# Far blocks' relative terms as rows of one product, and routed rows scattered to their tokens: a Macaron layer on one core

## The reference, cut to what matters

```python
x = x + 0.5 * ffn(layernorm(x), ...)          # x: 16 sequences x 512 tokens x 128
x = x + attention(layernorm(x), ...)
x = x + 0.5 * ffn(layernorm(x), ...)

def attention(hidden_states, ...):            # 16 heads of 8
    dist = jnp.clip(arange(s)[:, None] - arange(s)[None, :], -128, 128) + 128
    rel_pos = rel_emb[dist]
    scores = einsum('bhqd,bhkd->bhqk', q, k) + einsum('bhqd,qkd->bhqk', q, rel_pos)
    attn = softmax(scores / sqrt(8))
    local_ctx = einsum('bhqk,bhkd->bhqd', attn, v)
    ...                                       # a linear global part, gated; then Wo

def ffn(x_aD, ...):                           # 8192 tokens, 8 experts, F = 256
    topv, topi = top_k(x_aD @ router_DE, 2)
    gates = sigmoid(scores of the two chosen experts, -inf elsewhere)
    for each expert e: out_e = (silu(g x W_in[e]) * (g x W_swiglu[e])) @ W_out[e]
    return shared_ffn(x_aD) + sum over e of out_e
```

## Time and profile before

| | |
|---|---|
| median of three runs | 2360.72 us |
| the profiled execution | 2373.01 us |
| its span, first to last instruction | 2371.2 us |
| granted TensorE clock, mean | 0.934 |
| busy: PE, VectorE, ScalarE, GpSimd | 2056.5, 1517.5, 1417.9, 1163.2 us |
| phases: load and ffn1, attention, ffn2 | 0 to 480, 480 to about 1835, 1835 to 2371 us |

### The profile page before, as it was taken

How to read it: one execution, slowest core, us unless ns; L and a number is a source line. 1 busy time by engine, 2 the same in 40 slices (tenths; PEclk the granted TensorE clock), 3 DMA queues, 4 the chain that set the end, 5 groups by cost and what they waited for, 6 DMA issues and landing times. The chain is left out here.

```text
span 2371.2 us, 49029 instructions
## 1 busy us (share of the span) xinstructions
PE 2056.5 (87%) x16104; PEld 1440.3 (61%) x16104; DVE 1517.5 (64%) x4212; ACT 1417.9 (60%) x2771; POOL 1163.2 (49%) x1525
## 2 busy tenths in 40 slices
PE   4777899849999999999999999999999777799850
PEld 3555677626666666666666666666665555667640
DVE  7775556636767767776766666666664766555641
ACT  3655566626666666666667666666774555566540
POOL 0776004446665656555654545455531277400676
PEclk9878999958999999999999999999999888999985
DMA  5355878668887888888878888888882114677862
GB/s 133 128 195 205 243 238 260 215 175 235 237 234 231 242 224 247 241 236 230 250 222 233 247 244 241 229 239 244 240 240 78 32 51 161 193 242 242 269 202 75
DMA packets 293456, 493.53 MB, mean 208 GB/s; under 512 B 42452, under 2 KB 196948, under 8 KB 293204
## 3 DMA queue, kind: packets, MB, share of 16 engines
q1 hardware_dynamic: 237364, 309.26, 46.8%
q0 software_dynamic: 53248, 180.01, 23.5%
q10 hardware_dynamic: 2592, 1.13, 0.2%
HBM read 252.56 MB, written 210.89 MB: 195 GB/s over the span
## 5 line engine op out<-in xcount | busy, mean ns | idle before, releaser
L1422 DVE CUSTOM_DVE_ANT_0 at_junk<-at_ps_s,at_rel 128x512 bf16<-128x512 f32 x1024 | 664.5, 686 | 238.0 <-PE at_ps_s L978 209.6
L1153 ACT ACTIVATE at_probs<-at_ps_t 128x512 f32<-128x512 f32 x1024 | 558.0, 598 | 94.1 <-PE at_ps_t L963 81.5
L1162 ACT COPY at_src<-at_ps_r 128x512 f32<-128x512 f32 x512 | 302.1, 590 | 360.9 <-PE at_ps_r L992 258.0
L963 PE MATMUL at_ps_t<-tab_ident,at_rel 128*128 128x128 f32 x3328 | 483.8, 285 | 0.0
L963 PEld LDWEIGHTS at_ps_t<-tab_ident,at_rel 128*128 128x128 f32 x3328 | 361.2, 143 | 69.3 <-issue 2.0
L509 POOL DMA_INDIRECT rows_x<-ffn_xe,rows_index x256 | 263.7, 1030 | 180.7 <-ACT ffn_xe L461 103.1
L519 POOL DMA_INDIRECT ffn_zg<-rows_z,rows_home x176 | 177.0, 1006 | 349.4 <-issue 349.4
L720 DVE TENSOR_TENSOR ffn_h<-ffn_silu,ffn_ps_gate 128x512 f32<-128x512 f32 x248 | 170.5, 687 | 259.7 <-ACT ffn_silu L482 259.1
L1006 PE MATMUL at_ps_v<-at_probs,at_v 128*32 128x256 f32 x4096 | 330.6, 395 | 0.2 <-ACT at_probs L1153 0.2
L978 PE MATMUL at_ps_s<-at_ks,at_qs 31*128 31x512 f32 x1024 | 307.6, 504 | 3.9 <-DVE at_mx L1422 2.3
L482 ACT ACTIVATE ffn_silu<-ffn_ps_mid 128x512 f32<-128x512 f32 x248 | 148.8, 600 | 243.9 <-PE ffn_ps_gate L321 243.4
(11 more groups left out here) (204 smaller groups left out, 3438.1 us busy)
## 6 DMA issues: line engine op xcount, KB each, us to landing
at_band<-at_src POOLq DMA_DIRECT2D x192, 574.0 KB, 4.9
at_rel<-at_band SPq DMA_DIRECT2D x512, 143.5 KB
ffn_w_expert<-rows_w SPq DMA_DIRECT2D x92, 768.0 KB, 5.1
at_band<-at_src POOLq DMA_DIRECT2D x64, 512.0 KB, 5.1
ffn_xg<-rows_x SPq DMA_DIRECT2D x92, 256.0 KB, 3.9
rows_z<-ffn_y SPq DMA_DIRECT2D x92, 256.0 KB, 5.4
rows_x<-ffn_zero SPq DMA_DIRECT2D x46, 256.0 KB, 3.2
at_rel<-at_band SPq DMA_DIRECT2D x64, 128.0 KB
```

The costliest lines, as they stand in the source:

```text
L963: ins = pe.matmul(ps_t[:, i, HALF * n + P * l:HALF * n + P * (l + 1)], rel[:, c % RREL, l, 2 * hp + i, kb * P:(kb + 1) * P], ident[:], sta ...
L1153: act.activation(probs[:, kp, 2 * hp + i].rearrange("p n q -> p (n q)"), ps_t[:, i, :], ACT.Exp).then_inc(exp_done.sem, 1)
L1162: act.copy(src[:, l, 2 * hp:2 * hp + 2, 0:BAND], ps_r[:, :, 0:BAND]).then_inc(qr_out.sem, 1)
L1422: dve.tensor_tensor_reduce(out=junk[:, i, :], in0=ps_s[:, i, :], in1=rel[:, c % RREL, l, h, :], scale=1.0, scalar=-3e38, op0=ALU.add, op1= ...
```

## The change

It has two parts.

**Attention.** For the first two query blocks, the far keys to the right (distance clipped at the other end) get their relative term from the stack. One product per sequence of the queries with a table `wf` (the difference of the two end rows, by head; three matmuls of 16 x 256) gives the term for 256 queries and 16 heads; VectorE splits it into a high and a low part in the unused rows of `k32`, and SP sends it by four transfers into spare rows of `qs`, for which `ks` has ones from the first far key on. The transposes of the far blocks are skipped, `fill_far` stops at the end of the near blocks, and the rest of `rel` is zero. The far product takes V's place at (2, 2); V goes to (3, 3) and its copy to (4, 0).

**FFN.** Every row sent to an expert carries one more number, the row of `rows_t` at which its output belongs (token and choice; rows of padding have a spare number). In ffn2 VectorE takes these numbers from the loaded tile (`take_ids`), GpSimd scatters `y` with them, four indirect DMAs of 128 rows per job (`scatter_out`), instead of SP's store; and SP loads the tiles back by two plain transfers (`load_back`), tiles 0 to 9 in the last jobs, 10 to 15 after them. ffn1 carries the numbers too but gathers as before.

```diff
+                t = n - FIRST_B[1] - 7
+                return t if n < JOBS and GROUPS[0][0] <= t < GROUPS[0][1] else None
...
+            return 16 * 2 * (T if first else 1) * (t // RZ + 1)
+
+        def z_written(n):
+
+            return 16 * (1 if first else T) * (b_of(n) // 2 + 1)
...
+                    if not first:
+                        sp.wait_ge(ids_done, b_of(n - RG) + 1)
...
+            def load_back(t):
+
+                last = FIRST_B[0 if t < CUT else 1] + TILES[0 if t < CUT else 1] - 1
+                for n in (last - 1, last):
+                    sp.wait_ge(z_out[n % 2], z_written(n))
+                if t >= RZ:
+                    sp.wait_ge(z_added, t - RZ + 1)
+                for k in range(2):
+                    at = k * TOKENS + t * W
+                    sp.dma_start(zg[:, t % RZ, k], rows.t[at:at + W].rearrange("(p c) d -> p c d", p=P)).then_inc(z_in[t % RZ], 16)
...
-                if NA <= n - 4 < JOBS:
+                if first and NA <= n - 4 < JOBS:
                     store_rows(n - 4)
+                if not first and gathered_at(n + 1) is not None:
+                    load_back(gathered_at(n + 1))
                 if store is not None and gathered_at(n - 1) is not None:
                     store_result(gathered_at(n - 1))
             if store is not None:
-                for t in LATE:
+                for t in LATE[:RZ]:
+                    load_back(t)
+                for i, t in enumerate(LATE):
                     store_result(t)
+                    if i + RZ < len(LATE):
+                        load_back(LATE[i + RZ])
...
-                    act.wait_ge(z_out[m % 2], 16 * (b_of(m) // 2))
+                    act.wait_ge(z_out[m % 2], z_written(m - 2))
...
+                    act.copy(xe[:, t % RX, :, :, D:D + 1].rearrange("p k s a -> p k (s a)"), ids[:, t])
...
+            def scatter_out(n):
+                pool.wait_ge(y_done, b_of(n) + 1)
+                pool.wait_ge(ids_done, b_of(n) + 1)
+                for c in range(T):
+                    pool.indirect_dma_start(rows.t, bass.IndirectOffsetOnAxis(row_ids[:, n % RI, c, :], 0),
+                                            y[:, n % 2, c, :], None).then_inc(z_out[n % 2], 16)
...
+            else:
+                for n in range(NA, JOBS):
+                    scatter_out(n)
...
+            def take_ids(n):
+                dve.wait_ge(rows_in[n % RG], 16 * rows_loads(n))
+                if b_of(n) >= RI:
+                    dve.wait_ge(z_out[n % 2], z_written(n - RI))
+                drawn = xg[:, n % RG, :, D:D + 1].rearrange("p c a -> p (c a)")
+                dve.tensor_scalar(beside[:, n % RI], drawn, float(2 * TOKENS), float(W * (n % RI)), ALU.is_ge,
+                                  ALU.mult).then_inc(ids_step, 1)
+                dve.wait_ge(ids_step, b_of(n) + 1)
+                dve.tensor_tensor(row_ids[:, n % RI].rearrange("p c a -> p (c a)"), drawn, beside[:, n % RI],
+                                  ALU.add).then_inc(ids_done, 1)
...
-    PROJECT_V, V_OUT = (2, 2), (2, 3)
+    PROJECT_V, V_OUT = (3, 3), (4, 0)
     QUERIES_IN = ((2, 0), (2, 0), (2, 1))
     KEYS_IN = ((3, 0), (3, 1), (3, 0))
+    FAR_PROJECT, FAR_OUT, FAR_IN = (2, 2), (2, 3), (3, 0)
...
-                            if kb < qb - 1:
+                            if kb < qb - 1 or kb > qb + 1:
...
+                    far_ring, n = seq_ring(far_in, c // PER)
+                    pe.wait_ge(far_ring.sem, far_ring.at(n + 1, 0))
...
+                    pe.wait_ge(far_done.sem, far_done.at(b, 2))
+                elif slot == 4 and b is not None:
...
+                elif place == FAR_PROJECT:
+                    pe.wait_ge(qlo_done.sem, qlo_done.at(b, 1))
                     pe.wait_ge(k32_done.sem, k32_done.at(b, 1))
                     maximum_left(c)
                     if e is not None:
                         pe.wait_ge(o_step.sem, o_step.at(e, 8))
+                    for i, (w, q) in enumerate(((wf_hi, q_hi), (wf_hi, q_lo), (wf_lo, q_hi))):
+                        ins = pe.matmul(misc[0:H, 0:HALF], w[:], q[:, 0:HALF], start=(i == 0), stop=(i == 2))
+                    ins.then_inc(far_prod.sem, 1)
+                elif place == PROJECT_V:
+                    pe.wait_ge(far_done.sem, far_done.at(b, 2))
+                    maximum_left(c)
+                    if e is not None:
+                        pe.wait_ge(g_step.sem, g_step.at(e, 6))
...
-                            pe.wait_ge(v_done.sem, v_done.at(coming(c), 1))
+                            pe.wait_ge(far_done.sem, far_done.at(coming(c), 2))
...
-                        pool.tensor_copy(rel[:, c % RREL, l, :, key:S],
-                                         far[:, c % RREL, l].broadcast_to([P, HG, S - key])).then_inc(fill_done.sem, 1)
+                        end = P * (2 * half_of(c) + l + 2)
+                        pool.tensor_copy(rel[:, c % RREL, l, :, key:end],
+                                         far[:, c % RREL, l].broadcast_to([P, HG, end - key])).then_inc(fill_done.sem, 1)
...
+                if place == FAR_IN:
+                    sp.wait_ge(far_done.sem, far_done.at(b, 2))
+                    far_ring, r = far_in[b % R2], b % R2
+                    for x in range(4):
+                        l, part = x // 2, x % 2
+                        at = (STEP * x + STEP - 1) * LINE + r * SETS * S + P * l
+                        to = bass.AP(qs[:].tensor, at, [[32 * LINE, HG], [S, SETS], [1, P]])
+                        src_at = HALF * part + P * l
+                        sp.dma_start(to.bitcast(F32), k32[0:H, src_at:src_at + P]).then_inc(far_ring.sem, 16)
...
+            for x in range(4):
+                far_from = HALF + P * (x // 2)
+                ones = bass.AP(ks[:].tensor, (STEP * x + STEP - 1) * LINE + far_from, [[32 * LINE, HG], [S, R2 * SETS], [1, S - far_from]])
+                sp.dma_start(ones.bitcast(F32), glob[0:32, 2:2 + (S - far_from) // P, :]).then_inc(extra_in.sem, 16)
...
+                elif place == FAR_OUT:
+                    high, low = (k32[0:H, HALF * part:HALF * (part + 1)].bitcast(F32R) for part in range(2))
+                    dve.wait_ge(klo_done.sem, klo_done.at(b, 1))
+                    dve.wait_ge(far_prod.sem, far_prod.at(b, 1))
+                    dve.tensor_copy(high, misc[0:H, 0:HALF]).then_inc(far_done.sem, 1)
+                    dve.wait_ge(far_done.sem, far_done.at(b, 1))
+                    dve.tensor_tensor(low, misc[0:H, 0:HALF], high.bitcast(F32), ALU.subtract).then_inc(far_done.sem, 1)
...
+                                dve.memset(rel[:, j, 0, :, 2 * P:S], 0.0).then_inc(rel_cleared.sem, 1)
                                 dve.memset(rel[:, j, 1, :, 0:P], 0.0).then_inc(rel_cleared.sem, 1)
+                                dve.memset(rel[:, j, 1, :, 3 * P:S], 0.0).then_inc(rel_cleared.sem, 1)
...
-        rows.x.append(dram(f"rows_x{g}", [tall, D]))
+        rows.x.append(dram(f"rows_x{g}", [tall, D + 1]))
         rows.z.append(dram(f"rows_z{g}", [(2 * tiles + E - 1) * ROWS_AT_ONCE, D]))
+    rows.t = dram("rows_t", [(2 * sum(GROUP_TILES) + 8) * ROWS_AT_ONCE, D])
```

103 lines of the change are left out of this document (70 added, 33 removed).

## The result

| | before | after |
|---|---|---|
| median of the runs | 2361.48 us (4 runs, 2360.05 to 2362.70) | 2323.91 us (4 runs, 2320.92 to 2326.26) |
| the profiled execution | 2373.01 us, span 2371.2 | 2320.92 us, span 2319.1 |
| ratio of the medians | | 0.984, interval 0.9817 to 0.9863 |

The change makes the kernel 37.6 us faster; 62 were predicted, and the range of 2262 to 2330 us holds the result. Two of the four executions of experiment 6, which took 2586.72 and 3327.58 us at granted clocks unlike the others, are left out everywhere.

What follows compares the result with a forecast made beforehand. Attention was taken as bound by TensorE's work, the second FFN's 80 us tail by GpSimd's gathers. Gains of 27 us in attention and 35 in the FFN made 62: 2360.7 - 62 = 2299 us, range 2262 to 2330.

Steps and rivals of the forecast that it cites:

- The upper bound of 83 us: Attention, even items: 768 transposes fewer at 0.108 us each save at most 83 us, with no stall coming in.
- 0.85 us a pair: Attention, last two steps of even items: each shortened pair saves 0.85 us, 54 us over 64 pairs.
- What is given back, 27 us in sum: Attention: costs of 6, 7, 9, 3 and 2 us taken off the 54 us saved, leaving 27 gained.
- Local outputs, 6 us: Attention, step 2 of slots 0 and 2: VectorE's reciprocal and product cost 0.2 us in 30 pairs, 6 us (0 to 16).
- Far rows on the band product's wait, 9 us: Attention, first step of slot 4: the next sequence's band products wait for four more transfers, 15 x 0.6 = 9 us.
- Low part of the keys, 3 us: Attention, early sequences: VectorE's far product copy out of PSUM waits for the keys' low part, 3 us (0 to 10).
- Late pieces, 7 us: Attention, step 3 in the first 68 slots: VectorE's additions cost 0.2 us in 34 pairs, 7 us (0 to 20).
- Collision at the start of the second stage, 9 us: Second FFN: the third output waits for the first one's scatters, behind GpSimd's first-stage sends; 9 us lost on ScalarE.
- Loads and stores in the last jobs, 5: Second FFN: group 0's ten direct loads and their stores fall in the last ten jobs, costing 5 us (0 to 12).
- The last rows land 14 us after the last output was due, and 17 for the tail: Second FFN's end: scatters lag closely spaced last jobs, 14 us (8 to 20); loading six tiles back, 17 (14 to 24).
- Rival C: Second FFN, second stage: scatters held by VectorE take 1.96 us each and bound it; slower, 2383 us, chance 0.04.
- Rival A: Attention gives nearly nothing: VectorE's loop and ScalarE set short steps, relative rows arrive late; gain 5 + 35, 2321 us, chance 0.13.

Runs made afterwards that it cites:

- experiment 6: The changed kernel with each query block's band sent out by two transfers of two heads: 2292.66 and 2315.18 us, no ratio given.
- 3: The kernel before with the far transposes left out and nothing in their place: 2521.46 us, ratio 0.9961 to the kernel before.
- 12: The changed kernel with the far transposes done all the same, adding zeros: 2495.78 us, ratio 0.9893 to the kernel before.
- 9: The changed kernel with the band sent in two transfers of two heads, run again on another chip: 2470.26 us, ratio 0.9813 to the kernel before.
- 11: The changed kernel with four output buffers instead of two in both FFN phases, on a third chip: 2467.20 us, ratio 0.9769 to the kernel before.
- 2: The kernel before with all FFN edits and none of the attention's: 2502.91 us against 2530.54, ratio 0.9889.
- 7: The kernel before with the band sent in two transfers of two heads: 2392.59 us, ratio 1.012 to the kernel before.
- 1: The kernel before with all attention edits and none of the FFN's: 2523.98 us against 2530.54, ratio 0.9955.
- 4: The changed kernel with four output buffers instead of two in both FFN phases, on the first of its chips: 2485.07 us, ratio 0.9832 to the kernel before.
- 5: The changed kernel once more, unedited, on another chip: 2322.67 us against 2364.28 for the kernel before, ratio 0.9806.
- 10: The changed kernel with the band in two transfers and four output buffers in both FFN phases: 2455.59 us, ratio 0.975 to the kernel before.
- experiment 8: The changed kernel with ScalarE's exponent of each step ahead of its half of the band copy: 2514.17 us, ratio 1.0626 to the kernel before.

## Why the prediction was right or wrong

### Where the attention's gain went

**The steps at full clock.** A sequence has 32 steps, eight slots of four, and each of them can be followed through the sequences: from one pair of score products to the next. At full clock the median length of a step agrees between the kernels to some 0.01 us wherever the edits don't touch it; step 3 of slots 4 and 7 varies by up to 1 us or more and is no measure by itself. These are medians over the steps that stood wholly at 2.4 GHz, in us; "late" are the sequences 9 to 14 (counted from 0), in which no late pieces are added, "early" 1 to 8:

| | before | after | skip alone (3) | additions alone (12) | band in halves (9) |
|---|---|---|---|---|---|
| slot 6, steps 2 and 3, late | 4.58 | 3.61 | 3.60 | 4.58 | 3.61 |
| slot 0, steps 2 and 3, late | 5.60 | 4.75 | 4.75 | 5.60 | 5.13 |
| the same, early | 5.60 | 5.10 | 5.10 | 5.60 | 5.10 |
| slot 2, steps 2 and 3, late | 5.68 | 4.41 | 4.82 | 5.15 | 4.41 |
| the same, early | 5.69 | 5.59 | 5.40 | 5.61 | 5.53 |
| slot 3, step 3, late | 2.69 | 3.65 | 2.75 | 3.59 | 3.59 |
| slot 3, steps 0 to 2, late | 6.33 | 6.46 | 6.55 | 6.32 | 6.33 |
| slot 7, late | 8.84 | 9.41 | 9.22 | 8.92 | 9.12 |
| slots 1 and 5, late | 17.99 | 17.97 | 17.99 | 17.97 | 17.98 |

Three things can be read from it. First, a pair that became short gives 0.97 us in slot 6 and 0.85 in slot 0 of a late sequence, as much as the prediction took. Second, the largest loss in an odd item is not a wait at all: step 3 of slot 3 is 0.9 us longer wherever V's product stands in it (after and 12, not 3), and about half of that left slot 2 (5.68 to 5.15 in experiment 12). One such step in the kernel after, 3.65 us instead of 2.70:

```profile
1390.03 1.10 PE L1042 MATMUL at_ps_s<-at_ks,at_qs 31*128 31x512 f32 x2
...
1392.13 1.06 PE L1149 MATMUL at_misc<-tab_wv,at_xT 128*128 128x128 f32 x8
...
1393.68 0.50 PE L1042 MATMUL at_ps_s<-at_ks,at_qs 31*128 31x512 f32 x2
```

Third, what the skip itself costs the odd items is 0.2 us in slot 3 and 0.4 in slot 7 of a late sequence (3 against before; in slot 7 of an early one 0.2 to 1.4, by kernel), and none in slots 1 and 5; the band in halves takes 0.1 and 0.3 of the change's own 0.13 and 0.57 back. So the chain seen above (the band copy waits for the transfer, the exponents stand behind the copy) is there, but it is small. Its wait is as large in sum as it was (87.5 us over 59 times before, here after; window 540 to 1820 us, columns as above), though there are fewer transposes to wait beside:

```profile
PEld at_ps_s L1042 <- DVE at_mx L1518: 137.9, 340, 3.1
...
ACT at_src L1239 <- DMA at_band<-at_src: 87.7, 70, 3.3
...
PE at_misc L1180 <- DVE at_k L1563: 8.9, 7, 2.4
```

**The clock.** What the steps gain at full clock isn't what was measured (18.9). TensorE, by windows, before and after (columns as in the first fence), then experiments 12 and 11, which differ in the 768 transposes and in the output buffers of the FFN:

```profile
600.00:1200.00 600.00, 587.71 (x5655) 387.14 (x5654) 428.43 (x1312) 398.55 (x737) 361.51 (x528) 0.99 0.84 237
1200.00:1770.00 570.00, 565.14 (x5594) 373.55 (x5592) 384.52 (x1204) 394.64 (x726) 281.55 (x447) 0.99 0.84 238
```

```profile
600.00:1200.00 600.00, 579.16 (x5398) 363.86 (x5397) 437.72 (x1342) 400.05 (x745) 327.79 (x530) 0.96 0.86 240
1200.00:1770.00 570.00, 558.92 (x5380) 352.37 (x5378) 396.06 (x1244) 399.32 (x741) 247.45 (x455) 0.98 0.85 244
```

```profile
660.00:1260.00 600.00, 588.04 (x5706) 385.46 (x5703) 437.00 (x1334) 402.34 (x741) 328.47 (x531) 0.99 0.86 240
```

```profile
660.00:1260.00 600.00, 581.50 (x5352) 362.28 (x5352) 436.43 (x1334) 398.27 (x740) 327.28 (x530) 0.94 0.85 238
```

With the transposes PE is busy for 588 us of the first 600 and the mean granted clock is 0.99; without them it is busy for 579 and 582, and the clock is 0.96 and 0.94. I added up the stretches in which the clock stands at its lower level, between the first and the last score product, without the one in which each kernel enters the phase (30 to 34 us more in every one of them):

| 1.2 GHz, us in sum | |
|---|---|
| all transposes: before, experiments 2, 7, 12 | 30.7, 37.5, 44.4, 20.5 |
| far ones skipped: after, experiments 1, 3, 4, 5, 11 | 88.7, 81.9, 95.6, 75.1, 95.6, 95.6 |
| skipped, band in halves: experiments 6, 9, 10 | 54.6, 61.4, 75.1 |
| skipped, exponents first: experiment 8 | 218.5 |

The first two groups don't overlap, and 3 against 2 and 12 against 11, whose attention programs differ in the skip alone, show that it is the skip that does it. One such stretch in the changed kernel, by windows, and its steps on TensorE:

```profile
1196.00:1211.50 15.50, 13.41 (x134) 7.96 (x127) 12.26 (x42) 11.16 (x21) 4.24 (x10) 1.00 0.75 216
1211.50:1218.30 6.80, 6.80 (x30) 3.85 (x28) 2.56 (x9) 4.66 (x8) 2.39 (x4) 0.50 0.58 176
1218.30:1234.00 15.70, 15.50 (x159) 9.88 (x159) 12.21 (x39) 10.80 (x20) 5.87 (x12) 1.00 0.80 225
```

```profile
1213.11 0.79 PE L1042 MATMUL at_ps_s<-at_ks,at_qs 31*128 31x512 f32 x2
...
1214.78 1.97 PE L1027 MATMUL at_ps_t<-tab_ident,at_rel 128*128 128x128 f32 x8
...
1218.92 0.50 PE L1042 MATMUL at_ps_s<-at_ks,at_qs 31*128 31x512 f32 x2
...
1219.48 1.10 PE L1027 MATMUL at_ps_t<-tab_ident,at_rel 128*128 128x128 f32 x8
...
1221.08 0.50 PE L1042 MATMUL at_ps_s<-at_ks,at_qs 31*128 31x512 f32 x2
```

Ahead of it stand four steps of two transposes, and PE is busy for 13.4 of the 15.5 us. Then the clock is at 0.50 for 6.8 us: eight transposes take 1.97 us instead of 1.10 (one step later, where the clock is back), and the step 1218.92 - 1213.11 = 5.81, instead of the 3.15 that the same step has in the other sequences.

What a microsecond at 1.2 GHz costs can be estimated by fitting to all steps of sequences 1 to 14 one length for each of the 32 steps, early and late apart, and one price per microsecond at 1.2 GHz. It comes out as 0.59 us before and 0.58 after; 0.56 to 0.79 in the kernels with all transposes (2, 7, 12), 0.43 to 0.54 in those without them (1, 3, 4, 5, 6, 9, 10, 11). By these prices, for a phase of 36 early and 28 late pairs of items:

| us gained | at full clock (estimate) | by the steps as they are | S |
|---|---|---|---|
| before to after | 50 | 21 | 18.9 |
| the attention part: 2 to 1 | 36 | 21 | 18.5 |
| the skip: 2 to 3 | 33 | 11 | 12.7 |
| the skip: 12 to 11 | 42 | 13 | 13.6 |

So 33 to 50 us are there at full clock, and 15 to 29 of them are gone with the clock. With one price of 0.4 to 0.6 for all kernels the first column is 35 to 56. The columns differ by nothing but the price times the low stretches, so that they fit together proves nothing; and a stall that both lengthens a step and comes with a fall of the clock is counted with the clock here.

That the skip lowers the clock is shown by the experiments; the price of 15 to 29 us is an estimate from the steps and not from a run of its own. A run that fills TensorE's gaps with idle products, which would separate the two, wasn't tried.

### Step by step

- **What bounds the kernel**: right. The attention stays with the loop of TensorE, VectorE and ScalarE, and the tail was GpSimd's.
- **The upper bound of 83 us**: the busy time fell by 78; the time by 13 to 14 (experiments 3 and 12).
- **0.85 us a pair**: the size held, 0.85 and 0.97 us at full clock in slots 0 and 6. The reading that it came from did not: "what a step of two really costs is shown in the odd items" sets steps at different places against each other, and a step's length depends on what else stands in it (at full clock an odd item's steps of two last 1.60 to 2.49 us, its steps of eight 2.15 to 3.16). The same place in both kernels is the measure.
- **The clock, a term that stands in the sum at nothing**: this is the step that failed. The prediction counted a saved transpose as saved time and a stall as a lost saving, and left out that the clock may fall more often when TensorE has less to do. The earlier trace rows gave the clock as 0.99, and I took it as given for after. The runs show 89 us at 1.2 GHz instead of 31, and by the estimate above 15 to 29 us lost by it.
- **What is given back, 27 us in sum**: too large. By the estimate above 36 to 50 us are left at full clock, of 54. Local outputs, 6 us: the pair in slot 0, which has them, gives 0.12 us less than that in slot 6, against the 0.2 taken. Far rows on the band product's wait, 9 us: that wait is 6.3 us once, at the start of the phase; the transfers land in time in all later sequences. Low part of the keys, 3 us: in step 3 of slot 2 TensorE waits at L1180 for VectorE's copy of the far product out of the shared PSUM tile, 8.9 us in the seven sequences 1 to 7 (the third line of the fence on waits), within the 0 to 10 given. Late pieces, 7 us: that wait is most of what the early pair of slot 2 lacks against the late one; in slot 0 it lacks 5.10 - 4.75 = 0.35, 3 us over nine sequences, within 0 to 20. V's own product "only moves": it costs 0.9 where it stands now and frees 0.5 in slot 2, and experiment 12 shows no net loss. Start-up, 2 us: 2.9.
- **Attention in all**: predicted -27, measured -16.7 (the three rows of the table). That the two are so near is in part luck: the clock's 15 to 29 us were missing on one side, and some 10 to 20 us too many were given back on the other.
- **Collision at the start of the second stage, 9 us**: right, 8.87 us at the place foretold, with the third output; in experiment 5's profile the longest such wait is 8.9 us as well. No experiment took the wait away where it stands (4, 10 and 11 ran on chips on which it doesn't show), so what it costs is read from these two traces. From the first output to the fourth it takes 27.2 us against 19.0. **Loads and stores in the last jobs, 5**: wrong by its sign. From the fourth output to the last it takes 236.6 us against 233.3 before, and the last two outputs' waits for scatters, 7.2, lie in that; without them it is 3.9 shorter.
- **The last rows land 14 us after the last output was due, and 17 for the tail**: the last output was 7.2 us late by its own waits, and the loads go out 2300.23 - 2290.65 = 9.6 after it, together 16.8; then 18.9. Both are a little too small. In sum 35 were predicted, and 38.8 measured from the phase's first tile to the end (1.1 lost in its first stage).
- **The first FFN, hidden, 0 to 5**: 3.4 us.
- **Rival C and the rule for it**: nothing of it. All scatters of the second stage:

```profile
L559 POOL DMA_INDIRECT rows_t<-ffn_y,ffn_row_ids x184: 962/967/1406, 2040.2 to 2297.9; - x184
```

The mean is 0.97 us and the pitch beside a busy VectorE 1.27 us (2040.21, 2041.48, 2042.75). The box in "SBUF: two separate sides" of the Trainium skill's "SBUF — State Buffer", by which a GpSimd DMA issue waits while VectorE runs a two-port operation, makes no difference here: VectorE is busy for 72 of 110 us in the window from 2180, and the longest issue of all takes 1.41 us. Whether VectorE's operations here are of the two-port kind no run shows. The sum went by the row, and the row was right.
- **Rival A** (attention gives nearly nothing, 2321 us) is nearest in time to 2324, but by another mechanism: score products wait for maxima 137.9 us, over the 120 that I had named as its sign, but before it was 129.6 already, so the sign was badly chosen. SP's four more issues do no harm.
- **The sum against the median**: 62 was taken off the median unscaled, while the profile of before was 11.5 us above it. Of the 24 us that were missing, 10 are in the stages (-52 against -62) and 14.5 are the two profiled executions' distance to their medians. Which stage has those can't be told without profiles of other executions.
